# Softmax shift written into the score banks by ScalarE, negative means on GpSimd, new step orders and banks: a fused convolution-attention and transformer kernel

## The chip, the cores and the metric

One Trainium2 chip, one of its cores. The time is the device time of one execution in microseconds (us). TensorE (PE, with PEld for its weight loads), VectorE (DVE), ScalarE (ACT), GpSimd (POOL) and SyncE (SP) run their own instruction queues in order and meet at semaphores. The Python source was written with the step order of each engine as a table.

## The reference

32 images of 128 channels and 32x32 positions (1024 tokens) run through three layers, each with a residual:

```python
# L0: group norm, then attention over all 1024 tokens of an image, one head of 128
h = group_norm(x, gn_w, gn_b)
q, k, v = split(einsum('oc,bcn->bon', qkv_w, h) + qkv_b)
attn = softmax(einsum('bcn,bcm->bnm', q, k) * C ** (-0.5), axis=-1)
x = x + (proj_w @ einsum('bcm,bnm->bcn', v, attn) + proj_b)
# L1: layer norm, attention in windows of 32 tokens with 8 heads, out-projection,
#     layer norm, relu(x @ w1.T + b1) @ w2.T + b2, layer norm, residual
t = t + L1_attn(layer_norm(t))
# L2: layer norm, quantise to fp8 e4m3, matmul with a quantised kernel, bias, residual
t = t + L1_ffn(layer_norm(t))
```

The change touches the softmax of the first attention: its scores are shifted by the row maximum before the exponential.

## The kernel before

An image is worked on in two halves of 512 tokens. Each engine has a list of steps `name:half` in `PROGRAM`; `-` and `--` after a step say that it works for the image one or two iterations back, so three images are in flight at once. `@b` in TensorE's list names the PSUM bank (0 to 5) of the step's output; banks 6 and 7 hold the accumulators of the global products (`PV_BANKS`). The tables repeat per image: TensorE's as a loop of the hardware, the others written out. Before a TensorE step writes into its bank, `claim` (L861) waits for the semaphore with which the bank's last holder was read out (`RELEASE`, L97). In this table the order is written by hand or by a planner outside of the kernel; nothing is decided at run time, and an engine whose next step waits holds up all steps behind it.

The softmax of the global attention, for each image:

- `max:0` to `max:15` (TensorE L939, VectorE L710): rough scores, query-major, in one fp16 matmul of 128x512; VectorE takes the row maximum. Eight of them cover a half of the queries.
- `maxima:h` (VectorE L712): reduces them to `cmax`, one value per query, and splits it into a bf16 high and low part in columns 0 and 1 of `cparts`.
- `shift:h` (TensorE L942): turns `cparts` in four bf16 transposes, so that rows 0 and 1 hold the two parts for 512 queries; ScalarE (L519) copies these two rows into `shift`, whose other rows are zero.
- `st:0` to `st:15` (L952): one score tile each, keys on the partitions, 512 queries along the row. TensorE first multiplies `minus` (all -1) with `shift` (L962), which puts the negative maximum into the bank, and adds three matmuls of fp16 high and low halves (`three`, L873 to L877). ScalarE's `st` (L524) takes the exponential into one of four `p32` buffers (`PRING`).
- `pv:0` to `pv:15` (L966): fp32 products of `p32` with the values, four of 128x129 each; the profile records each of these twice. The last one of a half lets VectorE add the residual (`t`, L740).

Layer norms are VectorE's `variance` (L744: statistics, mean and variance, then epsilon in `veps`, then the negative mean `nmean`), GpSimd's `power` (L382: `rstd` by `pow`, then `nshift`), and four passes of ScalarE (`normalise`, L498), after which TensorE turns the result (`turn_in`, `turn_mid`). There are eight per image. Projections, window attention and the feed-forward part go in the same pattern: TensorE writes a bank, ScalarE reads out a high half in fp16 (`qh`, `xh`, `kk`, `oh`), VectorE the low half (`ql`, `xl`, `ol`), TensorE uses both.

## Time and profile before

| | |
|---|---|
| time, median of 3 runs | 2333.63 us (2331.12 to 2341.1) |
| the profiled execution, its own time | 2340.18 us |
| its span | 2338.4 us |
| TensorE busy | 2203.6 us, 94% |
| VectorE busy | 1748.5 us, 75% |
| ScalarE busy | 1476.5 us, 63% |
| GpSimd busy | 1219.1 us, 52% |
| granted TensorE clock, mean | 0.986 |

The busy time of an engine is that in which any of its instructions runs. TensorE's matmuls overlap: a row of 512 columns is shown with 0.38 us, but the next starts after 0.215 us, so the spacing of starts is what a matmul costs in a dense stretch. An idle time in square brackets is that of the engine in front of the row, with what ended it.

### The profile page before, as it was taken

To read this page: it belongs to the slowest core of one execution; us is meant where nothing else is said; L and a number is where in the kernel's file an instruction comes from. 1 tells how busy PE (TensorE), PEld (TensorE's weight loads), DVE (VectorE), ACT (ScalarE), POOL (GpSimd) and SP (SyncE) were. 2 spreads that over 40 slices of the span, in tenths; PEclk is the share of its full clock that TensorE was granted. 3 is DMA by queue.
4 is the path that set the end of the run, shared out by engine and by line. 5 is a ranking of instruction groups with operands and counts; after the bars stand their busy time and mean duration, and the time that the engine had idled before them with its cause. 6 is when DMAs were issued, how large, how long until landed. Compare 5 with 4: busy or idle time off the path is not lost.

```text
span 2338.4 us, 59675 instructions
## 1 busy us (share of the span) xinstructions
PE 2203.6 (94%) x21902; PEld 1605.9 (69%) x21902; DVE 1748.5 (75%) x5668; ACT 1476.5 (63%) x2881; POOL 1219.1 (52%) x1323
## 2 busy tenths in 40 slices
PE   4899999999999999999999999999999999999974
PEld 3677766677776677776677777677777677767653
DVE  5677787777787877787777787777787787787753
ACT  2566666766666666666766666666666666666653
POOL 5255444555444555444555454555555555555544
PEclk8999999999999999999999999999999999999997
DMA  1111111111111111111111111111111111111110
GB/s 44 29 36 30 45 38 45 30 40 29 44 37 45 29 41 30 44 37 45 36 36 31 43 36 45 42 31 34 39 36 45 44 28 38 34 36 45 37 28 19
DMA packets 76181, 86.79 MB, mean 37 GB/s; under 512 B 20624, under 2 KB 55440, under 8 KB 76048
## 3 DMA queue, kind: packets, MB, share of 16 engines
q1 hardware_dynamic: 62368, 52.44, 9.4%
q10 hardware_dynamic: 13680, 33.04, 4.2%
q14 instruction: 106, 0.87, 0.1%
q8 instruction: 27, 0.44, 0.1%
HBM read 18.29 MB, written 16.78 MB: 15 GB/s over the span
## 4 chain that ended last, share of the span: by engine, by line
PE 77%; ACT 7%; DVE 6%; issue 4%; SPq 2%; DMA 2%; POOL 2%; ACTq 0%; POOLq 0%; DVEq 0%
PE ps L981 16%; PE ps L875 10%; PE ps L1077 9%; PE ps L877 9%; PE ps L876 9%; PE ps L1045 5%; PE ps L962 4%; PE ps L939 4%; PE ps L1027 4%; PE ps L993 2%; ACT y L498 2%; SPq L328 2%; PE ps L928 1%; PE ps L1097 1%; DMA ptbd<-et 1%
## 5 line engine op out<-in xcount | busy, mean ns | idle before, releaser
L981 PEld LDWEIGHTS ps<-vg,p 128*128 128x128 f32 x4096 | 506.1, 192 | 40.5 <-issue 6.4
L385 POOL TENSOR_TENSOR rstd<-veps,halfpow 128x4 f32<-128x4 f32 x256 | 260.0, 1016 | 508.5 <-DVE veps L755 508.5
L981 PE MATMUL ps<-vg,p 128*128 128x129 f32 x4096 | 523.6, 277 | 0.9 <-ACT p L529 0.9
L529 ACT ACTIVATE p<-ps 128x512 f32<-128x512 f32 x512 | 292.1, 589 | 143.0 <-PE ps L877 113.0
L710 DVE TENSOR_REDUCE cm<-ps 128x1 f32<-128x512 f32 x512 | 334.9, 680 | 16.5 <-PE ps L939 16.3
L419 POOL TENSOR_TENSOR e<-e,srec 128x512 f32<-128x512 f32 x128 | 134.2, 1049 | 246.2 <-DVE srec L798 246.0
L1077 PE MATMUL ps<-w,hid 128*128 128x128 f32 x2048 | 241.7, 276 | 1.8 <-ACT hid L581 1.7
L1077 PEld LDWEIGHTS ps<-w,hid 128*128 128x128 f32 x2048 | 236.2, 192 | 7.6 <-issue 1.8
L581 ACT ACTIVATE hid<-ps,cols 128x512 f32<-128x512 f32 x256 | 165.9, 685 | 97.0 <-PE ps L877 96.9
L939 PE MATMUL ps<-kgh,qgh 128*128 128x512 f16 x512 | 175.8, 384 | 28.6 <-DVE qgl L704 22.3
L962 PE MATMUL ps<-shift,minus 128*128 128x512 bf16 x512 | 194.5, 380 | 2.0
L876 PE MATMUL ps<-qgl,kgh 128*128 128x512 f16 x512 | 194.5, 380 | 0.0
L875 PE MATMUL ps<-qgh,kgh 128*128 128x512 f16 x512 | 194.5, 380 | 0.0
L877 PE MATMUL ps<-qgh,kgl 128*128 128x512 f16 x512 | 194.4, 380 | 0.0
L403 POOL TENSOR_TENSOR y<-y,rows 128x512 f32<-128x512 f32 x64 | 81.6, 1275 | 133.5 <-PE ps L993 133.5
L572 ACT ACTIVATE oh<-ps 128x512 f16<-128x512 f32 x64 | 38.2, 597 | 178.2 <-PE ps L1045 178.2
L765 DVE TENSOR_TENSOR xl<-ps,xh 128x512 f16<-128x512 f32 x128 | 88.5, 692 | 76.9 <-ACT xh L537 76.8
L829 DVE TENSOR_TENSOR w<-ps,res 128x512 f32<-128x512 f32 x64 | 44.3, 692 | 127.4 <-PE ps L1077 124.3
L1045 PE MATMUL ps<-ptbd,v 128*32 128x128 f32 x4096 | 134.1, 277 | 3.0 <-DMA ptbd<-et 2.5
L498 ACT ACTIVATE y<-y,nshift,rstd 128x128 f32<-128x128 f32 x256 | 105.1, 482 | 42.8 <-POOL nshift L392 42.8
L498 ACT ACTIVATE z<-u,nshift,rstd 128x128 f32<-128x128 f32 x256 | 105.1, 482 | 35.9 <-POOL nshift L392 35.9
L1045 PEld LDWEIGHTS ps<-ptbd,v 128*32 128x32 f32 x4096 | 107.2, 111 | 26.2 <-DMA ptbd<-et 11.4
(184 smaller groups left out, 5504.3 us busy)
## 6 DMA issues: line engine op xcount, KB each, us to landing
ptbd<-et SPq DMA_DIRECT2D x512, 64.0 KB, 2.1
kbd<-kk SPq DMA_DIRECT2D x512, 32.0 KB, 2.0
out_y<-o_sb ACTq DMA_DIRECT2D x64, 256.0 KB, 2.4
x_sb<-in_x ACTq DMA_DIRECT2D x31, 512.0 KB, 4.0
x_sb<-in_x SPq DMA_DIRECT2D x1, 512.0 KB, 3.4
e<-in_w_t SPq DMA_DIRECT2D x1, 256.0 KB, 3.3
w<-in_w_t SPq DMA_DIRECT2D x1, 256.0 KB, 3.2
hid<-in_in_w_t SPq DMA_DIRECT2D x1, 192.0 KB, 2.6
```

The source lines that it names most:

```text
L385: g.tensor_tensor(rstd[:, k, h, :], veps[:, k, h, :], halfpow[:], ALU.pow).then_inc(s[f"ln_pow{k}"], 1)
L498: last = sc.activation(dst[:, h, P * j:P * (j + 1)] if dst is z else dst[:, h, j, :], src[:, h, j, :], ACT.Identity, bias=nshift[:, k, h, ...
L529: sc.activation(p32[:, c % PRING, :], bank("st", c), ACT.Exp, scale=C ** -0.5).then_inc(s["p_made"], 1)
L710: v_.reduce_max(cm[:, c // 2, c % 2:c % 2 + 1], bank("max", c), X).then_inc(s["max_out"], 1)
L875: mm(dst, lhi, rhi, start=first, stop=False, **kw)
L876: mm(dst, lhi, rlo, start=False, stop=False, **kw)
L877: return mm(dst, llo, rhi, start=False, stop=last, **kw)
L939: mm(bank("max", c), qgh[:, P * (c // 2):P * (c // 2 + 1)], kgh[:, HALF * (c % 2):HALF * (c % 2 + 1)], start=True, stop=True).then_inc(s[" ...
L962: mm(bank("st", c), minus[:], shift[:, h, :], start=True, stop=False)
L981: last = mm(ps[:, b, at:at + PVW], p32[:, c % PRING, part], vg32[:, j, :], start=j == 0 and q % 2 == 0, stop=j == MT - 1, skip_group_check ...
L1045: last = mm(ps[WIN * two:WIN * (two + 1), BANK["pv0", h], P * j:P * (j + 1)], v32[:, h, odd, j, WIN * two:WIN * (two + 1)], ptbd[:, h, j, ...
L1077: last = mm(bank("down", h)[:, part], hid[:, f, part], w2[:, f, :], start=f == 0, stop=f == FT - 1)
```

## The change

1. **Shift.** `maxima` is the reduction to `cmax` alone. `shift:h` turns each column of `cmax`, spread over 128 columns, in fp32 (four transposes), so that every partition holds the maxima of the 512 queries. ScalarE copies the whole bank, negated, into `shift`, now fp32 with 128 rows.
2. **Seeds.** A new step of ScalarE, `seed:c`, copies `shift` into the bank of score tile `c`. `st:c` on TensorE waits for it and adds its three matmuls, none of which starts the bank afresh; the matmul with `minus` is gone. Score tiles have banks 0 and 1 to themselves, in turn; a seed waits until the exponential of the tile two before has been taken. All other steps share banks 2 to 5. Once at the start two fp32 matmuls write to banks 0 and 1.
3. **Negative means.** `nmean` is computed by GpSimd at the head of `power`, instead of by VectorE behind `veps`.
4. **Orders and banks.** All tables of `PROGRAM` are new.

```diff
 PV_BANKS = (6, 7)
+ST_BANKS = (0, 1)
 PROGRAM = {
     "pe": """
-        max:7@3- turn_x:0@4- v:1@5-- out:0@2-- q:1@1-- shift:0@0- turn_x:1@3- max:8@2- st:0@4- max:9@0- st:1@3-
+        shift:0@5- out:0@2-- turn_x:0@3- max:9@5- st:0@0- st:1@1- max:10@4- pv:0- score0:1@2-- score1:1@5-- st:2@0-
...
+def seeded_over(c):
+    if c >= len(ST_BANKS):
+        return 0, c - len(ST_BANKS)
+    return 1, max(d for d in range(2 * MT) if d % len(ST_BANKS) == c)
...
-        cparts = sb("cparts", [P, HT, P], BF16)
-        shift = sb("shift", [P, 2, HALF], BF16)
+        shift = sb("shift", [P, 2, HALF])
...
             def power(n, k, h):
+                pool.wait_ge(s[f"ln_mv{k}"], upto(n))
+                g.tensor_scalar(nmean[:, k, h, :], mv[:, k, h, :, 0], -1.0, None, ALU.mult).then_inc(s[f"ln_mean{k}"], 1)
                 pool.wait_ge(s[f"ln_veps{k}"], upto(n))
...
             def make_shift(kind, img, c):
                 act.wait_ge(s["shift_turned"], upto(img, c + 1, per=2))
-                sc.activation(shift[0:2, c, :], bank("shift", c)[0:2, 0:HALF // 2].bitcast(BF16),
-                              ACT.Copy).then_inc(s["shift_made"], 1)
+                sc.activation(shift[:, c, :], bank("shift", c), ACT.Copy, scale=-1.0).then_inc(s["shift_made"], 1)
+
+            def seed(kind, img, c):
+                act.wait_ge(s["shift_made"], upto(img, c // MT + 1, per=2))
+                back, last = seeded_over(c)
+                if due(value := upto(img - back, last + 1, per=2 * MT)):
+                    act.wait_ge(s["p_made"], value)
+                sc.activation(bank("st", c), shift[:, c // MT, :], ACT.Copy).then_inc(s["seed_made"], 1)
...
-                v_.reduce_max(cmax[:], cm[:, HT * c:HT * (c + 1), :], X).then_inc(s["cmax_made"], 1)
-                dve.wait_ge(s["cmax_made"], upto(img, c + 1, per=2))
                 if due(value := upto(img, c, per=2)):
                     dve.wait_ge(s["shift_turned"], value)
-                v_.tensor_copy(cparts[:, :, 0], cmax[:]).then_inc(s["chi_made"], 1)
-                dve.wait_ge(s["chi_made"], upto(img, c + 1, per=2))
-                v_.tensor_tensor(cparts[:, :, 1], cmax[:], cparts[:, :, 0], ALU.subtract).then_inc(s["cparts_made"], 1)
+                v_.reduce_max(cmax[:], cm[:, HT * c:HT * (c + 1), :], X).then_inc(s["cmax_made"], 1)
...
-                v_.tensor_scalar(nmean[:, k, h, :], mv[:, k, h, :, 0], -1.0, None, ALU.mult).then_inc(s[f"ln_mean{k}"], 1)
...
+                if isinstance(img, int) and img == 0 and c == 0:
+                    pe.wait_ge(s["const_made"], 6)
+                    for b in ST_BANKS:
+                        mm(ps[:, b, :], identf[:], vg32[:].rearrange("p a b -> p (a b)")[:, 0:HALF], start=True, stop=True)
                 for q in range(HT):
-                    last = nc.tensor.transpose(dst[:, P * q:P * (q + 1)], cparts[:, q, :], identh[:])
+                    last = nc.tensor.transpose(bank("shift", c)[:, P * q:P * (q + 1)], cmax[:, q:q + 1].to_broadcast([P, P]),
+                                               identf[:])
...
             def st(kind, img, c):
                 h, j = divmod(c, MT)
-                claim(kind, img, "st", c)
+                pe.wait_ge(s["seed_made"], upto(img, c + 1, per=2 * MT))
...
-                mm(bank("st", c), minus[:], shift[:, h, :], start=True, stop=False)
                 three(bank("st", c), kgh[:, keys], kgl[:, keys], qgh[:, queries], qgl[:, queries],
-                      first=False).then_inc(s["st_mm"], 1)
+                      first=False, skip_group_check=True).then_inc(s["st_mm"], 1)
```

Three places of the new order. A row is a line of the kernel (of its own version), an instruction, and out<-in by the names of the code; `ps` is PSUM.

TensorE in the loop, from behind the turn of the first half's maxima to the first global product; before (L939 is `max`, L962 with `minus`, L875 to L877 the three matmuls of a score tile, L981 `pv`):

```order
L939 MATMUL ps<-kgh,qgh 128x512
L962 MATMUL ps<-shift,minus 128x512
L875 MATMUL ps<-qgh,kgh 128x512
L876 MATMUL ps<-qgl,kgh 128x512
L877 MATMUL ps<-qgh,kgl 128x512
L939 MATMUL ps<-kgh,qgh 128x512
```

And now (L949 is `max`, L993 `pv`):

```order
L949 MATMUL ps<-kgh,qgh 128x512
L885 MATMUL ps<-qgh,kgh 128x512
L886 MATMUL ps<-qgl,kgh 128x512
L887 MATMUL ps<-qgh,kgl 128x512
L885 MATMUL ps<-qgh,kgh 128x512
L886 MATMUL ps<-qgl,kgh 128x512
L887 MATMUL ps<-qgh,kgl 128x512
L949 MATMUL ps<-kgh,qgh 128x512
L993 MATMUL ps<-vg,p 128x129 x4
```

The first two score tiles now follow each other, each one matmul shorter, and a single `max` stands between them and the first product.

ScalarE at the same place; before (L521 the copy of the shift, L487 the turned x, L542 `qh`, L529 the exponential of a score tile, L561 the values, L498 a normalisation):

```order
L521 ACTIVATE shift<-ps 2x512
L487 ACTIVATE xt<-ps 128x512
L542 ACTIVATE qh<-ps,cols 128x512
L529 ACTIVATE p<-ps 128x512
L561 ACTIVATE v<-ps 128x16x16 x2
L529 ACTIVATE p<-ps 128x512
L498 ACTIVATE y<-y,nshift,rstd 128x128 x4
```

And now (L530 the shift, L537 a seed, L544 the exponential, L496 the turned x, L507 a normalisation):

```order
L557 ACTIVATE qh<-ps,cols 128x512
L530 ACTIVATE shift<-ps 128x512
L537 ACTIVATE ps<-shift 128x512 x2
L544 ACTIVATE p<-ps 128x512
L537 ACTIVATE ps<-shift 128x512
L544 ACTIVATE p<-ps 128x512
L537 ACTIVATE ps<-shift 128x512
L496 ACTIVATE xt<-ps 128x512
L507 ACTIVATE y<-y,nshift,rstd 128x128 x4
```

Two seeds stand behind the shift, then a seed behind each of the first exponentials; `qh` has moved ahead of the shift, the values behind.

VectorE ahead of the same turn; before (L710 a row maximum, L779 `kk`, L812 `ol`, L715 to L722 the maxima step, L818 the residual of the out-projection):

```order
L710 TENSOR_REDUCE cm<-ps 128x1 x3
L779 SCALAR_TENSOR_TENSOR kk<-ps,cols,kk 128x512
L710 TENSOR_REDUCE cm<-ps 128x1
L812 TENSOR_TENSOR ol<-ps,oh 128x512
L710 TENSOR_REDUCE cm<-ps 128x1
L715 TENSOR_REDUCE cmax<-cm 128x4
L720 CAST cparts<-cmax 128x4
L722 TENSOR_TENSOR cparts<-cmax,cparts 128x4
```

And now (L719 `kgl`, L725 a row maximum, L789 `kk`, L733 the maxima step, L822 `ol`):

```order
L719 SCALAR_TENSOR_TENSOR kgl<-ps,cols,kgh 128x512
L725 TENSOR_REDUCE cm<-ps 128x1 x2
L789 SCALAR_TENSOR_TENSOR kk<-ps,cols,kk 128x512
L725 TENSOR_REDUCE cm<-ps 128x1 x4
L733 TENSOR_REDUCE cmax<-cm 128x4
L822 TENSOR_TENSOR ol<-ps,oh 128x512
```

The last four row maxima follow each other, the maxima step is one instruction, and `ol` comes behind it.

## Rows read from the trace of the kernel before

**Rows 1.** Page, part 1: busy us of each engine (share of the span), instructions.

```profile
PE 2203.6 (94%) x21902; PEld 1605.9 (69%) x21902; DVE 1748.5 (75%) x5668; ACT 1476.5 (63%) x2881; POOL 1219.1 (52%) x1323
```

**Rows 2.** Windows: length, PE PEld DVE ACT POOL busy, clock; timeline, one image apart.

```profile
1004.00:1073.86 69.86, 68.15 (x686) 49.78 (x684) 53.94 (x177) 46.04 (x91) 37.22 (x41) 1.00 0.14 38
...
1004.41 0.30 PE L1097 MATMUL ps<-identf,u 128*128 128x128 f32 x1 [0.17 <-ACT qt L586]
1074.27 0.30 PE L1097 MATMUL ps<-identf,u 128*128 128x128 f32 x1 [0.17 <-ACT qt L586]
```

**Rows 3.** Timeline, TensorE, first score tile: start us, us, engine, line, operation, tiles, count.

```profile
1016.23 0.38 PE L939 MATMUL ps<-kgh,qgh 128*128 128x512 f16 x1
...
1016.67 0.38 PE L962 MATMUL ps<-shift,minus 128*128 128x512 bf16 x1
1016.88 0.38 PE L875 MATMUL ps<-qgh,kgh 128*128 128x512 f16 x1
...
1017.53 0.38 PE L939 MATMUL ps<-kgh,qgh 128*128 128x512 f16 x1
```

**Rows 4.** Timeline, TensorE: four bf16 turns, four fp32 turns, the next step.

```profile
1041.83 0.39 PE L947 MATMUL ps<-identh,cparts 128*128 128x128 bf16 x4
1042.05 0.60 PE L993 MATMUL ps<-identf,y 128*128 128x128 f32 x4
1042.49 2.04 PE L981 MATMUL ps<-vg,p 128*128 128x129 f32 x16
```

**Rows 5.** Page, part 5: the matmul with minus; count, busy us, mean ns.

```profile
L962 PE MATMUL ps<-shift,minus 128*128 128x512 bf16 x512 | 194.5, 380 | 2.0
```

**Rows 6.** Timeline, ScalarE behind the shift; page, part 5: Exp from SBUF to SBUF.

```profile
1015.98 0.59 ACT L521 ACTIVATE shift<-ps 2x512 bf16<-2x512 bf16 x1 [1.73 <-PE ps L947]
1016.48 0.57 ACT L487 ACTIVATE xt<-ps 128x512 f32<-128x512 f32 x1
...
L567 ACT ACTIVATE e<-e 128x512 f32<-128x512 f32 x128 | 80.4, 628 | 42.3 <-DVE e L788 41.9
```

**Rows 7.** Timeline, VectorE: the maxima step and the next; the negative mean and the next.

```profile
1014.73 0.16 DVE L715 TENSOR_REDUCE cmax<-cm 128x4 f32<-128x8 f32 x1
...
1015.22 0.69 DVE L818 TENSOR_TENSOR y<-ps,y 128x512 f32<-128x512 f32 x1
...
1017.35 0.16 DVE L756 TENSOR_SCALAR nmean<-mv 128x4 f32<-128x4 f32 x1
1017.42 1.28 DVE L710 TENSOR_REDUCE cm<-ps 128x1 f32<-128x512 f32 x2
```

**Rows 8.** Lines: GpSimd's nshift; count, busy us, mean ns, idle us before.

```profile
L392 POOL TENSOR_TENSOR nshift<-nmean,rstd 128x4 f32<-128x4 f32 x256 | 53.7, 210 | 20.2 <-POOL rstd L389 0.2
```

**Rows 9.** Timeline and window: last global products of an image to the next turn of maxima.

```profile
1067.01 2.95 PE L981 MATMUL ps<-vg,p 128*128 128x129 f32 x24
1069.79 0.22 PE L875 MATMUL ps<-wh,hh 128*128 128x128 f16 x1
...
1080.22 1.88 DVE L710 TENSOR_REDUCE cm<-ps 128x1 f32<-128x512 f32 x3
1082.01 0.75 DVE L779 SCALAR_TENSOR_TENSOR kk<-ps,cols,kk 128x512 f16<-128x512 f32 x1
1082.68 0.68 DVE L710 TENSOR_REDUCE cm<-ps 128x1 f32<-128x512 f32 x1
...
1085.42 0.39 PE L947 MATMUL ps<-identh,cparts 128*128 128x128 bf16 x4
...
1069.79:1085.42 15.63, 14.24 (x176) 9.37 (x174) 14.98 (x41) 10.38 (x20) 7.07 (x7) 1.00 0.21 56
```

**Rows 10.** Timeline, TensorE's waits in such a stretch; line L498, what its waits ended with.

```profile
1006.33 0.82 PE L939 MATMUL ps<-kgh,qgh 128*128 128x512 f16 x3 [0.61 <-DVE qgl L704]
1008.43 0.66 PE L993 MATMUL ps<-identf,y 128*128 128x128 f32 x4 [0.61 <-ACT y L498]
...
  POOL nshift L392: 90.6, 70
```

More of the change, by code:

```diff
@@ L63 @@
-    "act": """
-        vg:1- bias_x:0- k:1-- pv1:0-- turn_x:0- shift:0- turn_x:1- q:1-- st:0- v:1-- st:1- norm_mid:0-- turn_mid:0--
-        score0:1-- up0:0-- st:2- score1:1-- up1:0-- up2:0-- up3:0-- load_x:0 st:3- st:4- pv1:1-- st:5- norm_out:0--
-        st:6- norm_mid:1-- shift:1- st:7- turn_mid:1-- up0:1-- up1:1-- up2:1-- up3:1-- quant:0-- st:8- norm_in:0-
-        st:9- turn_in:0- st:10- norm_out:1-- k:0- turn_q:0-- st:11- st:12- ffn:0-- q:0- quant:1-- gn2:0 st:13-
-        st:14- st:15- score0:0- score1:0- kg:0 vg:0 kg:1 qg:0 turn_q:1-- v:0- qg:1 ffn:1-- norm_in:1- turn_in:1-""",
+        vg:1@2- max:2@5- k:1@4-- max:3@3- pv0:0@2-- max:4@5- max:5@3- max:6@4- pv1:0-- max:7@5- max:8@3- q:1@4--
@@ new lines @@
+        shift:0@5- out:0@2-- turn_x:0@3- max:9@5- st:0@0- st:1@1- max:10@4- pv:0- score0:1@2-- score1:1@5-- st:2@0-
+        pv:1- turn_mid:0@3-- st:3@1- max:11@2- max:12@5- v:1@4-- up0:0@3-- up1:0@2-- up2:0@4-- up3:0@3-- st:4@0-
+        turn_x:1@4- down:0@3-- pv0:1@4-- pv1:1-- st:5@1- pv:2- out:1@2-- pv:3- max:13@5- st:6@0- max:14@2- pv:4-
+        st:7@1- max:15@4- pv:5- pv:6- turn_mid:1@5-- shift:1@3- pv:7- up0:1@3-- up1:1@4-- up2:1@5-- up3:1@2--
+        st:8@0- gn1:0@5 down:1@2-- pv:8- st:9@1- turn_in:0@3- st:10@0- pv:9- gn2:0@3 k:0@2- st:11@1- v:0@4- pv:10-
@@ new lines @@
+        st:12@0- q:0@4- pv:11- st:13@1- pv:12- pv:13- st:14@0- st:15@1- turn_q:0@2-- score0:0@5- score1:0@4- pv:14-
+        pv:15- ffn:0@2-- kg:0@4 qg:0@3 turn_q:1@2-- qg:1@5 ffn:1@2-- vg:0@2 max:0@4 kg:1@3 turn_in:1@4- max:1@5""",
+    "dve": """
+        ln_in:1-- kg:0- qg:0- turn_p0:0-- prob1:0-- max:0- qg:1- turn_p1:0-- max:1- turn_in:1-- kg:1- max:2- max:3-
+        k:1-- max:4- max:5- max:6- max:7- maxima:0- pv1:0-- max:8- q:1-- out:0-- max:9- max:10- score0:1--
+        score1:1-- prob0:1-- turn_mid:0-- max:11- turn_p0:1-- prob1:1-- turn_p1:1-- max:12- down:0-- pv1:1-- out:1--
+        max:13- gn0:0 max:14- max:15- maxima:1- turn_mid:1-- ln_q:0-- pv:7- ln_in:0- quant:0-- down:1-- gn1:0
+        turn_in:0- k:0- ln_q:1-- q:0- gn2:0 quant:1-- score0:0- score1:0- pv:15- prob0:0-""",
@@ new lines @@
+    "act": """
+        k:1-- pv1:0-- q:1-- shift:0- seed:0- seed:1- st:0- seed:2- st:1- seed:3- turn_x:0- norm_mid:0-- score0:1--
+        st:2- turn_mid:0-- seed:4- st:3- score1:1-- v:1-- up0:0-- up1:0-- up2:0-- up3:0-- seed:5- st:4- turn_x:1-
+        load_x:0 pv1:1-- seed:6- st:5- seed:7- norm_out:0-- st:6- norm_mid:1-- st:7- turn_mid:1-- shift:1- seed:8-
+        seed:9- up0:1-- up1:1-- up2:1-- up3:1-- quant:0-- st:8- seed:10- norm_in:0- st:9- turn_in:0- st:10- seed:11-
+        norm_out:1-- k:0- seed:12- st:11- v:0- st:12- seed:13- q:0- seed:14- st:13- seed:15- quant:1-- gn2:0 st:14-
+        turn_q:0-- st:15- score0:0- score1:0- ffn:0-- kg:0 turn_q:1-- qg:0 qg:1 ffn:1-- norm_in:1- kg:1 vg:0
+        turn_in:1- bias_x:0 vg:1""",
@@ L69 @@
     "pool": """
-        prob1:1-- keep:1-- norm_mid:0-- down:0-- out:1-- norm_out:0-- norm_mid:1-- ln_q:0-- ln_in:0- quant:0--
-        down:1-- norm_out:1-- bias_out:0- ln_q:1-- gn2:0 quant:1-- prob0:0- prob1:0- ln_in:1- bias_out:1- keep:0-
-        out:0- prob0:1-""",
+        prob1:0-- bias_out:1-- keep:0-- out:0-- prob0:1-- prob1:1-- norm_mid:0-- keep:1-- down:0-- out:1--
+        norm_out:0-- norm_mid:1-- ln_q:0-- ln_in:0- quant:0-- down:1-- bias_out:0- norm_out:1-- ln_q:1-- gn2:0
+        quant:1-- prob0:0- ln_in:1-""",
@@ L348, in prologue @@
             def prologue():
[L349 removed]
+                for tile, value in ((identf, 0.0), (identh, 0.0), (group_mean, 1.0 / GROUP), (halfpow, -0.5)):
                     g.memset(tile[:], value).then_inc(s["const_made"], 1)
[L351 removed]
+                pool.wait_ge(s["const_made"], 4)
                 for tile in (identf, identh):
@@ L361, in prologue @@
                                 pattern=[[GROUP, P // GROUP], [0, GROUP]], channel_multiplier=-1).then_inc(s["const_mask"], 1)
-                for tile, value in ((cparts[:], 0.0), (vg32[:], 1.0), (ones, 1.0), (shift[:], 0.0)):
+                for tile, value in ((vg32[:], 1.0), (ones, 1.0)):
                     g.memset(tile, value).then_inc(s["const_made"], 1)
```

32 lines of the change are left out of this document (7 added, 25 removed).

## The prediction

> **What bounds the kernel now.** I read the shares of busy time first: TensorE is busy 94% of the span, VectorE 75%, ScalarE 63%, GpSimd 52% [rows 1]. The loop over the 32 images is steady: the same fp32 turn of the last step starts 69.86 us after its like one image earlier [rows 2], and in that one image TensorE is busy 68.15 of 69.86 us, VectorE 53.94, ScalarE 46.04 and GpSimd 37.22, at the full granted clock (1.00). So the period of one image sets the time, and TensorE's own work sets most of the period. Busy time there includes the tails of matmuls, so I also look at starts: TensorE does wait in one stretch, between the last product of an image's global attention (its last start is before 1069.79) and the turn of the next image's row maxima (1085.42) [rows 9]. Inside the same stretch of the period before stand waits for VectorE's low half of the queries and for ScalarE's normalisation, 0.61 us each as shown beyond the tails [rows 10]. VectorE is busy 14.98 of these 15.63 us [rows 9]. So: one stretch of about 15.6 us bound by VectorE, and some 54 us bound by TensorE.
>
> **TensorE loses one matmul per score tile.** Matmuls of 512 columns in one chain start 0.215 us apart: 1016.67, 1016.88, and four of them until 1017.53 [rows 3]. The tile's matmul with `minus` is one of these four; there are 512 [rows 5]. Per image 16 x 0.215 = 3.44 us go. They lie on TensorE, mostly in the stretch where TensorE itself is the bound, so this is time off the path.
>
> **The turn of the maxima becomes fp32.** Four bf16 turns take 0.22 us (1041.83 to 1042.05), four fp32 turns 0.44 us (1042.05 to 1042.49) [rows 4]. Two such steps per image: +0.44 us. In sum TensorE has 3.44 - 0.44 = 3.0 us less to do per image, 96 us over 32 images. Trainium skill, "FP8 and Floating Point Precision", section "TensorE Precision Notes", says that true FP32 takes four passes through the array. Four times the bf16 turn would be 0.88 us for a step, so +1.32 us per image instead of +0.44, 28 us in all; the fp32 turns of [rows 4] show twice, not four times.
>
> The new turns read one column spread over 128 (stride 0) as the stationary operand; no row shows that. The load of weights overlaps the matmul before it, so below I leave it at nothing, above at a doubled step: +0.9 us per image. The two fp32 matmuls at the set-up come once and cost under 2 us.
>
> **ScalarE gets 16 seeds per image.** A seed reads fp32 in SBUF and writes 128x512 fp32 to a PSUM bank. ScalarE writing PSUM isn't in the trace. The nearest rows: a 128x512 pass out of PSUM started 0.50 us before the next (1015.98, 1016.48), the Exp from SBUF to SBUF takes 0.628 us [rows 6]. I take 0.50, nearer in kind (a Copy of this width, queued back to back), and keep 0.63 as the upper end and 0.45 as the lower. 16 x 0.50 = 8.0 us (7.2 to 10.1). ScalarE goes from 46.0 to about 54 (53 to 56) of some 67 us, 80 to 84%: covered by TensorE as long as each seed is out when its bank is needed. If that cover is gone, 8 us a period lie bare. The Trainium skill, "ScalarE: Activation LUTs", section "Step-by-step: what each stage is for", says that ScalarE writes faster to PSUM than to SBUF; no row here shows it, and it would only make the seeds cheaper. The copy of the shift itself stays one instruction; 128 partitions instead of 2 cost the same, since the row with 2 partitions takes 0.59 like the full ones [rows 6].
>
> **VectorE loses small things.** The maxima step's three links take from 1014.73 to the next instruction at 1015.22 [rows 7], 0.49 us; one is left, some 0.1: two steps save 0.8 us per image. The negated mean costs 0.07 us from its start to the next one (1017.35, 1017.42) [rows 7], eight per image: 0.56. Together 1.4 us of 53.9.
>
> **GpSimd gets the negated mean**, 8 per image at 0.21 us (`nshift` has the same size) [rows 8], 1.7 us on an engine with 37.2 of 69.9. It now stands ahead of the `pow`. It starts with the mean and variance, while VectorE still adds epsilon, which covers about 0.17 of it; I take +0.1 us on each normalisation's chain, 0 to 0.25 as bounds. Only those that TensorE waits for matter (two or three per image), 0.2 us; what is queued behind a GpSimd wait is the next chain or the products of that half, which have room.
>
> **The new orders, walked.** I laid the new order of each engine out with starts and spacings of the old trace (0.50 per ScalarE pass [rows 6], 0.60 per row maximum and 0.67 per low half [rows 9], 0.1 to 0.2 per hand-over), from the last product of an image on.
> - The VectorE stretch. Between that product and the turn of the maxima VectorE has: the residual 1.25, two probability sums 1.74, the statistics 1.34, four low halves 2.6, two transposes 1.2, one `xl` 0.6, one `kk` 0.66, eight row maxima 4.8, the maxima 0.2, sum 14.4, with a few tenths of waiting 14.7; before, the same account gives 15.0, the trace 14.98 [rows 9]. So the stretch takes about 15.0 instead of 15.63 us. But the new order puts only about 11.9 us of TensorE's work there, where the old one had about 13.3. The waiting grows by about 0.8 us. Banks add nothing new to that in my walk, although all other tiles now share four banks: `max:3`, `vg:1` and `k:1` wait for banks 3, 2 and 4 within the same waiting.
> - Shift, seed, first tile. From the end of the turn to the first score tile: hand-over 0.2, shift 0.5 to 0.6, seed 0.5 to 0.6, 0.1, in sum 1.5. TensorE has out-projection 0.67, turn of x 0.45, one row maximum 0.22 between, 1.34. A wait of 0.2; the old order waited as long for the shift (the maximum at 1016.23 is followed by the tile at 1016.67, 0.22 late) [rows 3].
> - The other seeds stand ahead of their tile by the time of other steps on both engines. I find 0.15 us at `st:12` (behind a normalisation and a key step on ScalarE), 0.15 at `out:1`, nothing at `down:0`, and about 0.3 at `up0:1` as before. Against it the old wait of `turn_mid:0`, 0.3, goes, since more of TensorE's work stands ahead of it.
> Sum per image: 69.86 - 3.0 + 0.8 + 0.3 - 0.3 - 0.2 (tenths recovered where VectorE is shorter) = 67.45, about 67.4. Over 32 images 2.46 x 32 = 79 us. Start and end of the span stay. From the profiled run's own 2340.18 us (span 2338.4 and 1.8 around it) that gives 2261. The median of the runs before stands 0.28% lower (2333.63), so the forecast is 2255.
>
> **Rivals.**
> 1. **All of it.** The whole of TensorE's saving comes through: waits as before, 66.86 per image, 2340.2 - 96 = 2244, by the median 2238. For it: ScalarE has 20% free and the steps stand far from their seeds. Against it: the stretch that VectorE sets [rows 9]. With the waits even smaller it may reach 2225. Chance 0.17.
> 2. **Half of it.** VectorE's stretch and the four shared banks take another 1.0 to 1.5 us per image, 68.4 to 68.9, or 2287 to 2303. For it: a walk finds too few collisions, and a ScalarE at over 80% gives banks back later. Against it: outside the stretch the steps have other work between them. Chance 0.15.
> 3. **Slower.** Score tiles wait for seeds stuck in ScalarE's queue. ScalarE already sits idle before its normalisations waiting for GpSimd's `nshift`, 90.6 us in all [rows 10], 2.8 us per image, and now seeds for later tiles stand behind exactly these (`norm_out:1` ahead of `seed:12`, `norm_in:0` between `seed:10` and `seed:11`). TensorE stands at the tile, and with it all that is queued behind. Break-even is 3.0 / 16 = 0.19 us per tile; measurably slower from 0.21. At 0.25 us per tile the period is 69.86 + 4.0 - 3.0 = 70.9, the time 2340 + 32 = 2372, by the median 2366. Against it: most seeds are placed a whole tile or more ahead. Chance 0.07 for slower, 0.05 for the zone of no change.
> 4. **Dear turns.** The new turns cost what fp32 products do: 24 records, two to a matmul, in 2.78 us are 0.23 us each [rows 9], against 0.11 for a turn. 8 x 0.12 = 0.96 more per image, 31 us, 2286. For it: the spread column is a new operand. Against it: the same fp32 turn of other data [rows 4]. Chance 0.03. The Trainium skill's rule above would give nearly the same.
> 5. **The forecast,** 2240 to 2285: 0.53.
>
> **How the numbers follow.** About 0.5% is what a measurement of this kernel can tell from no change, 2322 to 2345. Faster: 0.53 + 0.17 + 0.15 + 0.03 = 0.88; within: 0.05; slower: 0.07. The range takes in rivals 1 and 2 and the bounds of seeds and turns: 2225 to 2305.
>
> **What would show it.** TensorE's records fall by 512, its busy time by 90 to 100 us; the seeds' row shows 512 passes of 0.55 to 0.63 us; ScalarE's busy time is near 1750 us, VectorE's near 1700; the period is 67 to 68 us; the stretch from the last product to the turn stays near 15 us and carries the longest waits; fp32 turns are spaced 0.11. Wrong would be: waits of score tiles for seeds of over 1 us per image in sum, seeds over 0.8 us, a granted clock under 1.00 in the loop, or a stretch over 16 us.

## The result, and the profile after it

The changed kernel takes 2315.05 us (median of 4 runs, 2311.32 to 2316.24); the kernel before, on the same chip, 2337.24. The ratio is 0.990, interval [0.988, 0.992]: faster by 22 us. The prediction was 2255, in 2225 to 2305. The direction was right; three quarters of the gain did not come, and the time lies above the range.

The page of the changed kernel, part 1, answers to [rows 1]:

```profile
PE 2141.3 (93%) x21394; PEld 1563.5 (68%) x21394; DVE 1698.6 (73%) x5284; ACT 1736.7 (75%) x3393; POOL 1272.5 (55%) x1576
```

TensorE has lost 508 records and 62.3 us of busy time, VectorE 50 us, ScalarE has gained 260: the work changed as forecast. Now the period, the time from the turn of the first half's maxima to the same turn one image later. Its median over the images is 69.30 us where it was 69.86. The first row below is one image of the changed kernel from turn to turn (length, then busy us of PE, PEld, DVE, ACT, POOL, clock), the second its stretch from the last global product of an image to the turn, as in [rows 9]:

```profile
1074.07:1143.35 69.28, 66.27 (x669) 48.55 (x669) 52.36 (x165) 54.13 (x107) 38.95 (x48) 1.00 0.14 38
1127.74:1143.35 15.61, 13.35 (x150) 7.45 (x148) 15.24 (x38) 10.39 (x19) 8.46 (x9) 1.00 0.26 73
```

The period fell by 0.56 us and not by 2.46. The stretch is 15.61 us in the median and not 15.0; it was 15.63. The rest of an image, between the turn and that last product, is 53.69 and was 54.23. I summed TensorE's starts to the next start over one image, each operation at its own usual spacing: its work did fall by 3.0 us, and what lies beyond the spacings rose by 2.4. The waits are new ones. TensorE's in the changed kernel (us in all, times, longest):

```profile
PE ps L1005 <- ACT y L507: 26.6, 33, 5.5
PE ps L885 <- ACT o_sb L609: 23.4, 30, 0.8
PE ps L885 <- DVE xl L775: 16.1, 64, 1.5
PE ps L1057 <- DMA ptbd<-et: 14.6, 29, 1.8
PE ps L1109 <- ACT qt L601: 13.1, 4, 11.3
PE ps L1098 <- POOL qz L438: 11.8, 30, 1.8
```

Before, the longest of these that came in every image were `y` 30.4 and `qgl` 22.3 us. `qgl` is gone; in its place `vg:0` waits in each image until ScalarE has read `ffn:1` out of the same bank (`o_sb`), 0.8 us, the probabilities' DMA (`ptbd`) and GpSimd's `qz` take 0.4 to 0.5 each, and the low half `xl` takes 0.25 twice in each image, where it had one wait in the whole run. Only once in 512 tiles did TensorE stand idle for a seed, 0.4 us.

### The profile page after: what moved, and what is told of

It reads as the page before. It is cut to its first block and busy times, and to the rows that moved or that the text cites. A ratio compares the mean times of both kernels' runs of the same rounds, so it can differ in the third digit from the quotient of the medians.

```text
span 2314.5 us, 59631 instructions
## 1 busy us (share of the span) xinstructions
PE 2141.3 (93%) x21394; PEld 1563.5 (68%) x21394; DVE 1698.6 (73%) x5284; ACT 1736.7 (75%) x3393; POOL 1272.5 (55%) x1576
## 5 line engine op out<-in xcount | busy, mean ns | idle before, releaser
L993 PEld LDWEIGHTS ps<-vg,p 128*128 128x128 f32 x4096 | 511.5, 192 | 51.9 <-issue 12.9
L993 PE MATMUL ps<-vg,p 128*128 128x129 f32 x4096 | 537.9, 278 | 0.7 <-ACT p L544 0.7
L392 POOL TENSOR_SCALAR nmean<-mv 128x4 f32<-128x4 f32 x256 | 58.3, 228 | 575.3 <-DVE mv L763 572.0
L544 ACT ACTIVATE p<-ps 128x512 f32<-128x512 f32 x512 | 300.2, 587 | 91.1 <-PE ps L887 90.6
L725 DVE TENSOR_REDUCE cm<-ps 128x1 f32<-128x512 f32 x512 | 334.0, 679 | 15.5 <-PE ps L949 13.9
L537 ACT ACTIVATE ps<-shift 128x512 f32<-128x512 f32 x512 | 300.9, 596 | 17.4 <-ACT p L544 0.7
L394 POOL TENSOR_TENSOR rstd<-veps,halfpow 128x4 f32<-128x4 f32 x256 | 265.8, 1038 | 0.0
L949 PE MATMUL ps<-kgh,qgh 128*128 128x512 f16 x512 | 176.8, 382 | 3.3 <-DVE kgl L719 1.6
L507 ACT ACTIVATE y<-y,nshift,rstd 128x128 f32<-128x128 f32 x256 | 105.2, 483 | 45.9 <-POOL nshift L401 45.9
L817 DVE STREAM_TRANSPOSE et<-e 128x512 f32<-128x512 f32 x128 | 90.4, 706 | 39.6 <-POOL e L428 38.9
```

What stands on the lines that cost most here:

```text
L394: g.tensor_tensor(rstd[:, k, h, :], veps[:, k, h, :], halfpow[:], ALU.pow).then_inc(s[f"ln_pow{k}"], 1)
L537: sc.activation(bank("st", c), shift[:, c // MT, :], ACT.Copy).then_inc(s["seed_made"], 1)
L544: sc.activation(p32[:, c % PRING, :], bank("st", c), ACT.Exp, scale=C ** -0.5).then_inc(s["p_made"], 1)
L725: v_.reduce_max(cm[:, c // 2, c % 2:c % 2 + 1], bank("max", c), X).then_inc(s["max_out"], 1)
L949: mm(bank("max", c), qgh[:, P * (c // 2):P * (c // 2 + 1)], kgh[:, HALF * (c % 2):HALF * (c % 2 + 1)], start=True, stop=True).then_inc(s[" ...
L993: last = mm(ps[:, b, at:at + PVW], p32[:, c % PRING, part], vg32[:, j, :], start=j == 0 and q % 2 == 0, stop=j == MT - 1, skip_group_check ...
```

## The experiments

Each was timed in three rounds beside the kernel before on its chip. "Ratio" is to the kernel before; the changed kernel has 0.990. The edits are against the changed kernel unless the kernel before is named. They are cut to what matters, and rows of `PROGRAM` are shown in part. Several runs test what their expectations call the ring or the section chain: the idea that a closed chain of hand-overs through all engines sets the period.

### Is TensorE the bound, or ScalarE with its seeds?

**Old order without `minus`** (kernel before):

```diff
-                mm(bank("st", c), minus[:], shift[:, h, :], start=True, stop=False)
                 three(bank("st", c), kgh[:, keys], kgl[:, keys], qgh[:, queries], qgl[:, queries],
-                      first=False).then_inc(s["st_mm"], 1)
+                      ).then_inc(s["st_mm"], 1)
```

> The kernel before, in its old order, with the matmul with minus left out of all 16 score tiles of an image (so the exponential is taken of unshifted scores); nothing else differs, ScalarE has no seeds. Theory of the section chain (mine now): an image's period is set by a ring of three pieces, the dense TensorE section from the turn of the first half's maxima to the end of down:1, then a chain of hand-overs through the norms and GpSimd to the last products, then VectorE's stretch. Only the 9 tiles st:0 to st:8 lie in the dense section, so at most 9 x 0.215 = 1.94 us per image come back, 45 to 62 us in all, ratio 0.973 to 0.981. Rival 'TensorE is the bound nearly everywhere and only the seeds or the new order cost': 16 x 0.215 x 32 = 110 us, ratio about 0.953.

2308.06 us, ratio 0.987 [0.986, 0.989]. Of 110 us of matmuls 30 come out as time. Both theories missed (45 to 62 us, or 110): whoever takes away TensorE's work alone, in the old order, gets about a quarter. The waits that grew against the kernel before are those for VectorE and for the keys' DMA (`kbd`, before 8.4 us, 7 times):

```profile
PE ps L939 <- DVE qgl L704: 27.9, 32, 1.6
PE ps L1026 <- DMA kbd<-kk: 23.2, 38, 4.0
```

**New order without seeds.** Three matmuls that start their bank afresh, no shift:

```diff
-"shift": make_shift, "seed": seed, "st": st
+"shift": make_shift, "st": st
-                pe.wait_ge(s["seed_made"], upto(img, c + 1, per=2 * MT))
+                claim(kind, img, "st", c)
...
-                      first=False, skip_group_check=True).then_inc(s["st_mm"], 1)
+                      ).then_inc(s["st_mm"], 1)
```

> The changed kernel without the 16 seeds (score tiles start their bank afresh and wait for the exponential of the tile two before instead; the scores stay unshifted). ScalarE has 8 us less per image. Section chain: the seeds stand in ScalarE's slack, at most 0.2 to 0.4 us per image come back, 2300 to 2312 us. Rival 'ScalarE's seeds ate the gain': most of the missing 60 us comes back, 2250 to 2270 us.

2312.53 us, 0.989 [0.988, 0.991]: all 512 seeds together cost about 3 us, which is within the noise. The rival with the seeds (3) is dead, and so is every story in which the 8 us of ScalarE's new work per image took the gain.

**One matmul less in the tiles `st:1` to `st:7`, or in `st:9` to `st:15`.** The edit of the first; the second has `c >= 9`:

```diff
+                if 1 <= c <= 7:
+                    mm(bank("st", c), kgh[:, keys], qgh[:, queries], start=False, stop=False, skip_group_check=True)
+                    mm(bank("st", c), kgl[:, keys], qgh[:, queries], start=False, stop=True,
+                       skip_group_check=True).then_inc(s["st_mm"], 1)
...
```

> The changed kernel with one of the three matmuls (the product with the low half of the queries) left out in st:1 to st:7, seven tiles in the dense TensorE section. 7 x 0.215 x 32 = 48 us less work for TensorE. Section chain: 30 to 48 us faster than the changed kernel, 2267 to 2285. Rival 'TensorE is off the path everywhere in the new order': under 10 us.

> The same with st:9 to st:15 instead, seven tiles behind down:1; TensorE's work falls by the same 48 us. Section chain: nothing, 0 to 8 us faster than the changed kernel, 2307 to 2316. If TensorE were the bound there too: 48 us faster, as in the run before.

2309.27 us (0.987 [0.986, 0.989]) and 2316.04 us (0.991 [0.989, 0.993]): 48 us of TensorE's work in either place are worth 6 us, not clear of the noise, and nothing. These tiles stand in "some 54 us bound by TensorE". The section chain had 30 to 48 us for the first of the two, and fell there; its rival, under 10, holds.

**One matmul more in each tile**, with zero weights:

```diff
+                mm(bank("st", c), zero[:], qgh[:, queries], start=False, stop=False, skip_group_check=True)
                 three(bank("st", c), kgh[:, keys], kgl[:, keys], qgh[:, queries], qgl[:, queries],
```

> The changed kernel with one matmul more in each score tile, of 128x512 with zero weights, so the result stays. It puts back 16 x 0.215 = 3.44 us of TensorE's work per image, 110 us in all, and nothing else of the old code. Theory A (TensorE's work is nearly on the path upwards, though taking more away brings nothing): 90 to 110 us slower than the changed kernel, ratio to before 1.028 to 1.037, so that nearly all of the 97 us between the old and the new code in the new order is this matmul. Theory B (the new order has slack of TensorE everywhere): under 50 us, ratio under 1.012, and the 97 us come mostly from the maxima step of VectorE.

2370.83 us, 1.014 [1.011, 1.017]: 110 us more of work cost 56. Between the two theories. So TensorE's work has a price of nothing to an eighth downwards and of half upwards: the changed kernel stands at a bend.

### Is it VectorE's row of maxima?

**Row maxima over half of the columns**, in the new order, in the old one, and in the old one without `minus`:

```diff
-                v_.reduce_max(cm[:, c // 2, c % 2:c % 2 + 1], bank("max", c), X).then_inc(s["max_out"], 1)
+                v_.reduce_max(cm[:, c // 2, c % 2:c % 2 + 1], bank("max", c)[:, 0:HALF // 2], X).then_inc(s["max_out"], 1)
```

> The changed kernel, but each row maximum of VectorE reads 256 of its 512 columns (the shift is then the maximum of half of the keys). VectorE's work falls by 16 x 0.27 = 4.3 us per image, 2.2 of it between the last product and the turn of the maxima; TensorE's and ScalarE's work is the same. The runs before showed that taking 1.5 us per image from TensorE gives 0.3 and 8 us from ScalarE 0.05. Theory of the ring: VectorE's unbroken row of work sets the stretch behind the last product, so 1.0 to 2.2 us per image come back, 2245 to 2285 us. Rival, TensorE or ScalarE set it: under 0.3 us per image, 2305 to 2315.

> The kernel before with the same halved row maxima, in the old order and with its matmul with minus. VectorE lighter by 4.3 us per image. If VectorE alone set the old order's period in its stretch, 1.0 to 2.0 us per image, 32 to 64 us faster than before (ratio 0.973 to 0.986). If TensorE set it, nothing (ratio 0.997 to 1.0).

> The kernel before with both cuts: no matmul with minus, halved row maxima. The matmul alone gave 0.93 us per image of its 3.44. If TensorE and VectorE hold the period together, the two cuts give more together than the sum of each alone: 3.0 us per image or more, ratio under 0.958. If a chain of hand-overs sets the rest, the sum stays about that of the two alone.

2296.48 (0.982 [0.980, 0.983]), 2333.95 (0.998 [0.997, 0.999]) and 2307.55 us (0.987 [0.985, 0.988]). VectorE's busy time falls by some 3.5 to 3.8 us per image each time (4.3 were expected). That brings 19 us in the new order, 4 in the old, and nothing in the old order once `minus` is gone. For the new order the 19 us, 0.55 per image, lie between the ring's 1.0 to 2.2 and its rival's 0.3. The window of one image of that last kernel (columns as above) still has TensorE busy 95%, with 3.44 us less to do; below it pieces of the chain of waits that ended last, in the same stretch (start, us, what):

```profile
2094.00:2162.85 68.85, 65.47 (x669) 48.29 (x668) 50.42 (x176) 45.66 (x91) 37.17 (x40) 1.00 0.14 38
```

```profile
2112.12 0.69 DVE xl L765
2112.81 0.60 DVE ssum L796
2113.44 0.26 DVE srec L798
2113.77 1.06 POOL e L419
2114.88 0.71 DVE et L807
2115.61 0.63 SPq L335
2116.28 0.61 SPq L335
2116.94 0.60 SPq L335
2117.58 4.08 DMA ptbd<-et
2121.80 1.95 PE ps L1044 x64
...
2130.09 0.90 DVE cparts L720
```

The chain goes through every engine and through the DMA: in one image of it, the 195 longest pieces sum to 32.1 us on TensorE, 15.8 on VectorE, 6.7 in transfers, 6.4 on ScalarE, 3.1 on SyncE, 1.6 on GpSimd. In the kernel before, the same sum over one image was 59.9 of some 68 us on TensorE. So a chain of hand-overs lay about 1 us per image behind TensorE's own: the period fell from 69.86 to 68.85 us and no further.

The last piece is one that the expectations did not count on. In the second half of each image the cast of the maxima step takes 0.89 us here, 0.54 in the old order without `minus` and 0.19 in the kernel before; it ends each time 0.03 us behind the same row of GpSimd. Where VectorE came to it sooner, it was held longer, and TensorE waited for the step at 30 turns (16.8 us, 12.3 of them at the start). That the lighter VectorE brought nothing there is in part this hold; how much of it, no run says.

**All three lighter** (no seeds, two of three matmuls in every tile, half maxima, as above):

> The changed kernel with all three engines lighter at once: no seeds (ScalarE 8 us per image less), two matmuls per score tile in all 16 (TensorE 3.44 less), halved row maxima (VectorE 4.3 less). Alone such cuts gave 0.05, 0.35 and 0.57 us per image. If two engines hold each other up (each relieved one meets the next), the three together give far more than the sum: 3 us per image or more, under 2225 us. If a ring of hand-overs of fixed latency holds the period: about the sum, 0.8 to 1.6 us per image, 2265 to 2290.

2284.38 us, 0.978 [0.975, 0.981]: 31 us below the changed kernel, about what the single effects sum to (3, 6 and 19), and in the ring's range. TensorE is busy 93% of an image even there, which shows how little that share tells; the window of one image, and TensorE's first waits:

```profile
1004.00:1072.25 68.25, 63.31 (x653) 46.84 (x652) 48.66 (x164) 45.71 (x91) 38.50 (x49) 1.00 0.14 39
...
PE ps L1041 <- DMA kbd<-kk: 41.7, 35, 2.6
PE ps L1007 <- ACT y L507: 41.0, 66, 5.5
```

### What the order costs, and what the code brings in it

**Old code in the new order** (kernel before, with all tables and banks of the changed one):

```diff
 PROGRAM = {
     "pe": """
-        max:1@1- max:2@2- max:3@0- vg:1@5- turn_in:1@3-- pv0:0@1-- max:4@2- max:5@5- k:1@4-- max:6@0- pv1:0--
+        vg:1@2- max:2@5- k:1@4-- max:3@3- pv0:0@2-- max:4@5- max:5@3- max:6@4- pv1:0-- max:7@5- max:8@3- q:1@4--
...
```

> The kernel before in all its code (matmul with minus, bf16 parts of the maximum, negative means on VectorE, no seeds), with the tables of orders and banks of the changed kernel. TensorE has 3.0 us more per image than the changed kernel, ScalarE 8 less, VectorE 1.4 more. If the new order only needs what the new code frees: slower than before, 71 to 72.5 us per image, ratio 1.01 to 1.035. If the new order is what makes the changed kernel faster and the seeds are worth little: 69.3 to 69.9, ratio 0.99 to 1.0.

2412.73 us, 1.032 [1.030, 1.034]. This is the run that splits the result: the new order by itself costs 75 us with the old code, and in the new order the new code is worth 98. Of the 2.4 us per image that the order costs, 2.3 lie outside of VectorE's stretch (56.49 against 54.23 us; the stretch is 15.73). That 98 is close to what the prediction counted on TensorE (96) is luck: much of it is not TensorE's work, as TensorE's longest wait shows:

```profile
PE ps L948 <- DVE cparts L723: 64.6, 63, 12.2
```

In the kernel before, TensorE waited for `cparts` once, at the start. Here it does so at 63 of the 64 turns, 0.8 us on average without the first. VectorE takes the maxima step right behind the last row maximum in both orders. In the kernel before, TensorE's other work just reached to the end of the step: the turn starts 0.24 to 0.26 us behind the last link, where the hand-over alone takes 0.15 in this run. In the new order TensorE comes too early at the first turn of an image (0.5 us), and at the second (1.2 us) the step is longer. VectorE and, below it, GpSimd at such a second turn (timeline):

```profile
1148.65 0.16 DVE L716 TENSOR_REDUCE cmax<-cm 128x4 f32<-128x8 f32 x1
1148.84 0.49 DVE L721 CAST cparts<-cmax 128x4 bf16<-128x4 f32 x1
1149.37 1.19 DVE L723 TENSOR_TENSOR cparts<-cmax,cparts 128x4 bf16<-128x4 f32 x1
...
1148.03 1.27 POOL L446 TENSOR_TENSOR u<-u,w 128x512 f32<-128x512 f32 x1
1149.26 1.26 POOL L412 TENSOR_TENSOR res<-y,rows 128x512 f32<-128x512 f32 x1
```

The cast ends with GpSimd's first row (1149.33 and 1149.30), the subtraction with its second (1150.56 and 1150.52). Each takes 0.18 us in the first half of an image, where no such row runs.

**The maxima step in three links**, in the changed kernel:

```diff
-                v_.reduce_max(cmax[:], cm[:, HT * c:HT * (c + 1), :], X).then_inc(s["cmax_made"], 1)
+                v_.reduce_max(cmax0[:], cm[:, HT * c:HT * (c + 1), :], X).then_inc(s["cm0_made"], 1)
+                dve.wait_ge(s["cm0_made"], upto(img, c + 1, per=2))
+                v_.tensor_copy(chi[:], cmax0[:]).then_inc(s["chi_made"], 1)
+                dve.wait_ge(s["chi_made"], upto(img, c + 1, per=2))
+                v_.tensor_tensor(cmax[:], cmax0[:], chi[:], ALU.max).then_inc(s["cmax_made"], 1)
```

> The changed kernel with the maxima step on VectorE in three links again (reduce, a cast of 128x4 to bf16, and a tensor_tensor of 128x4 with two operands in SBUF, here a maximum that leaves the shift valid). Nothing is left out. In the old code with the new order the last two links took 0.49 and 1.19 us in the second half of an image, while a 128x512 tensor_tensor of GpSimd ran, and TensorE waited 64.6 us for them. Theory A (the step is bare in the new order): they take the same here, the period grows by 0.5 to 1.7 us, ratio 0.997 to 1.014. Theory B (the freed TensorE time hides it): under 0.2 us per image, ratio 0.989 to 0.993.

2376.19 us, 1.017 [1.014, 1.019]: 61 us for 128 instructions that take 0.16 to 0.17 us each when nothing is in the way; the period is 71.03 us instead of 69.30, at the upper end of theory A. In the second half of an image they end with GpSimd's rows again (timeline, VectorE, GpSimd, and TensorE's turn that waits):

```profile
1061.72 0.59 DVE L736 CAST chi<-cmax 128x4 bf16<-128x4 f32 x1
1062.34 1.18 DVE L738 TENSOR_TENSOR cmax<-cmax,chi 128x4 f32<-128x4 f32 x1
...
1061.01 1.27 POOL L455 TENSOR_TENSOR u<-u,w 128x512 f32<-128x512 f32 x1
1062.24 1.26 POOL L421 TENSOR_TENSOR res<-y,rows 128x512 f32<-128x512 f32 x1
...
1063.67 0.62 PE L965 MATMUL ps<-identf,cmax 128*128 128x128 f32 x4 [1.50 <-DVE cmax L738]
```

So of the 98 us between the two codes the matmul alone is 56 and the maxima step alone 61. The two together were not run; if the rest of the new code (seeds, fp32 turns, means) is worth as little as the runs on it say, they overlap by about 20.

**`turn_x:0` moved into VectorE's stretch**, from behind the turn of the maxima to ahead of `pv1:0`:

```diff
-        pv0:0@2-- max:4@5- max:5@3- max:6@4- pv1:0-- max:7@5- max:8@3- q:1@4-- shift:0@5- out:0@2-- turn_x:0@3- max:9@5-
+        pv0:0@2-- max:4@5- turn_x:0@3- pv1:0-- max:5@3- max:6@4- max:7@5- max:8@3- q:1@4-- shift:0@5- out:0@2-- max:9@5-
```

> The changed kernel with one step moved: turn_x:0 from behind the turn of the maxima to ahead of it, between pv0:0 and pv1:0, where TensorE waits for VectorE anyway; ScalarE copies it there, in its 2.4 us of idle time, and no longer ahead of norm_mid:0. Nothing is left out. TensorE's dense piece from the turn of the maxima to turn_mid:0 (7.58 us) gets 0.45 shorter. Ring: 0.3 to 0.45 us per image faster, 2300 to 2306. If TensorE's place in the ring were not there (the runs that lightened it said 0.3 of 1.5): 0 to 0.1, 2312 to 2316.

2342.61 us, 1.003 [1.001, 1.004]: 28 us slower, where both theories had it faster. The stretch has no room even though TensorE idles in it. It is 16.74 us long instead of 15.61: the step takes a bank in turn, and TensorE waits for the row maxima to free the next. Besides, score tiles now do wait for a seed, 8.0 us in 32 times.

```profile
PE ps L936 <- DVE cm L712: 13.4, 34, 2.0
```

**`turn_mid:0` back to where the old order had it:**

```diff
-        score0:1@2-- score1:1@5-- st:2@0- pv:1- turn_mid:0@3-- st:3@1-
+        score0:1@2-- score1:1@5-- turn_mid:0@3-- st:2@0- pv:1- st:3@1-
     "act": """
-        seed:2- st:1- seed:3- turn_x:0- norm_mid:0-- score0:1-- st:2- turn_mid:0--
+        seed:2- st:1- turn_x:0- norm_mid:0-- seed:3- score0:1-- turn_mid:0-- st:2-
```

> The changed kernel with norm_mid:0 ahead of seed:3 on ScalarE and turn_mid:0 ahead of st:2 and pv:1 on TensorE, near to where the old order had it. Nothing is left out. In the changed kernel this turn starts 7.6 us after the turn of the maxima, in the kernel before 5.5. Theory A (the late turn_mid:0 is what the new order costs): it starts about 1 us earlier, down:0 too, and the period falls by 0.5 us or more, ratio under 0.985. Theory B (the stretch makes it up again, as it did when the score tiles behind it were made lighter): period within 0.3 us, ratio 0.986 to 0.995, with seed:3 later and TensorE waiting for the normalisation instead.

2337.04 us, 0.999 [0.998, 1.000], 22 us slower. The turn starts 7.06 us behind the turn of the maxima instead of 7.58, but now it is TensorE that waits, one time more per image (26.6 us, 33 times, in the changed kernel):

```profile
PE ps L992 <- ACT y L494: 58.1, 65, 5.5
```

The theory that the late place is the fault fell, and theory B, a period within 0.3 us, missed too. The late place suits the new order, perhaps because `out:0`, the head of that chain, comes behind the shift; that is not shown.

### Single hand-overs taken away

**`vg:0` behind `max:0` and `kg:1`; `vg:0` in the bank of `kg:0`** (banks 2 and 4 exchanged from there to `out:0`); **the first with the negative means on VectorE:**

```diff
-        ffn:1@2-- vg:0@2 max:0@4 kg:1@3 turn_in:1@4- max:1@5
+        ffn:1@2-- max:0@4 kg:1@3 vg:0@2 turn_in:1@4- max:1@5
```

```diff
-        ffn:1@2-- vg:0@2 max:0@4 kg:1@3 turn_in:1@4- max:1@5
+        ffn:1@2-- vg:0@4 max:0@2 kg:1@3 turn_in:1@2- max:1@5
```

> The changed kernel with one step of TensorE moved: vg:0, which waits in each image 0.78 to 0.94 us for ffn:1 to be read out of the same bank, comes behind max:0 and kg:1. Nothing is left out. Theory A (this new wait is where the gain went): the wait goes, the period falls by 0.8 us, 26 us in all, ratio to the kernel before near 0.979. Theory B (a ring of hand-overs: TensorE only arrives earlier at the next one, xl, qz, or the row maxima of VectorE): under 0.3 us per image, ratio 0.986 to 0.991, and the waits of other rows grow by about what this one loses.

> The changed kernel with the order kept and banks 2 and 4 exchanged from vg:0 to out:0, so that vg:0 gets the bank of kg:0 (free long before) and max:0, one step later, the bank of ffn:1. Nothing is left out. Theory A: about half of the wait goes (0.3 to 0.5 us per image), ratio 0.984 to 0.987. Theory B: under 0.2 us per image, ratio 0.988 to 0.991.

> The changed kernel with vg:0 behind max:0 and kg:1 and, besides, the negative means back on VectorE. Nothing is left out. If the two single effects add up (the second was 5 us alone): 5 us below the kernel with vg:0 moved alone. If TensorE and VectorE meet in the same hand-over at the row maxima, where VectorE's row is now the longer one, no gain beyond the kernel with vg:0 moved alone, or a loss of a few us, because the negated means (0.56 us per image) lie in VectorE's row.

2311.91 (0.990 [0.988, 0.993]), 2315.89 (0.991 [0.988, 0.993]) and 2312.88 us (0.990 [0.988, 0.993]); the period is 69.30, 69.28 and 69.22. The largest new wait, for `o_sb`, is gone from all three, and nothing is won, as theory B said. In the first it reappears at the next two hand-overs, 42.4 instead of 26.6 and 8.2 instead of 0.3, together what was taken away (23.4); in the second `y` has 47.3:

```profile
PE ps L998 <- ACT y L500: 42.4, 34, 5.5
...
PE ps L878 <- DVE qgl L712: 8.2, 31, 0.3
```

**Negative means back on VectorE; GpSimd's multiply with `RG2` left out:**

```diff
-                g.tensor_scalar(nmean[:, k, h, :], mv[:, k, h, :, 0], -1.0, None, ALU.mult).then_inc(s[f"ln_mean{k}"], 1)
+                v_.tensor_scalar(nmean[:, k, h, :], mv[:, k, h, :, 0], -1.0, None, ALU.mult).then_inc(s[f"ln_mean{k}"], 1)
```

```diff
-                g.tensor_tensor(w[:, h], w[:, h], row(RG2), ALU.mult).then_inc(s["t2a_made"], 1)
-                pool.wait_ge(s["t2a_made"], upto(n))
```

> The changed kernel with the negated mean back on VectorE behind veps, as before. VectorE has 0.56 us more per image, 0.2 of it in the stretch behind the last product; GpSimd 1.8 less, but its pow starts at the same time either way (0.25 us behind veps in both traces). Ring: 0.1 to 0.3 us per image slower, 2317 to 2325. If the move had lengthened the norms' chain: faster, 2300 to 2310.

> The changed kernel without GpSimd's multiplication of the second norm by its weight (1.27 us, twice per image; the result lacks that weight). GpSimd is busy only 55% of the span, so by busy time this is worth nothing. Ring of hand-overs: after down:1 its product is followed on GpSimd by the sum into u, then VectorE's statistics of u, and so on to the last products; one of the two multiplications stands in that chain, so up to 1.27 us per image come back, 0.5 to 1.3, 2275 to 2300 us. If the ring doesn't run through there: 2311 to 2317.

2310.33 (0.989 [0.986, 0.992]) and 2307.98 us (0.988 [0.985, 0.991]). The move of the means is worth nothing that can be told from zero: the loop's period is nearly the same (69.22), the 5 us in the profiled run lie ahead of the second turn of maxima at the start of the program (56.6 instead of 61.9 us). 1.27 us less on GpSimd per half image bring 7 us, between the ring's 16 to 42 and nothing.

None of the five stands clear of the changed kernel.

## Why the prediction was wrong, step by step

- **Removed work: right.** 3.44 and 0.44 us per image; TensorE's starts give 3.0. The fp32 turn takes 0.44 us (four turns at 1032.71, the next product at 1033.15), twice the bf16 turn of [rows 4], so the spread operand costs nothing and rival 4 is out. The rule of the Trainium skill, "FP8 and Floating Point Precision", section "TensorE Precision Notes", of four passes for fp32, is not borne out for turns; the fp32 products of [rows 9], 0.23 us each against 0.055 for a 16-bit one of 128 columns, do take four times as long.
- **Seeds: right in what matters.** 0.596 us each, 0.52 from start to start (two in 1.12); ScalarE is busy 75% of the span and 54.1 of 69.3 us in one image, as forecast. Without them 3 us less.
- **Negative means:** the +0.1 us on a normalisation's chain did not come; `rstd` starts 0.25 us behind `veps` in both kernels.
- **The step that failed first:** "one stretch of about 15.6 us bound by VectorE, and some 54 us bound by TensorE", and with it "mostly in the stretch where TensorE itself is the bound". A busy share near 94% and dense starts were taken for a bound. By the prediction's own terms these 54 us should have come down to 52.4 (67.4 less the stretch of 15.0); they came down from 54.23 to 53.69. The old order pays 30 us for 110 us of matmuls, the new one 6 and 0 for 48. Behind TensorE's row stood a chain through VectorE, GpSimd, SyncE, the transfers and ScalarE, about 1 us per image later, and [rows 10] had shown two of its waits in one place; the walk followed only the first tiles and the stretch, and held the rest for covered.
- **The new orders:** the sum gives them +0.8 us of waiting in the stretch and then tenths. With the old code they cost 75 us, 2.4 per image. The prediction never asked what the order does without the code. Where its own terms can be held against the trace: the stretch is 15.61 and not 15.0, with VectorE busy 15.24, 0.8 above the 14.4 of the walk, so 0.6 of the 1.9 us that are missing per image lie there. The other 1.3 lie outside of it, where the waits are hand-overs for which the sum has nothing (`vg:0` 0.8, `ptbd`, `qz` and `xl` 0.4 to 0.5 each).
- **VectorE's maxima step:** 0.4 us each, as work off a covered engine, and put into the sum as a tenth or two. In the new order TensorE stands idle for it, and in the second half of an image its two links are held by GpSimd's rows: 61 us. Without this piece the change would have been a loss: the kernel with three links takes 2376.
- **Start and end stay:** nearly. The third turn of maxima comes 1.8 us earlier, the end 3.7 us sooner behind the last turn: 5.5 of the 24 us between the two profiled spans.

Rival 2 had the right kind ("a walk finds too few collisions") and too small a size, 68.4 to 68.9 us per image against 69.30. That no single engine's work sets the period is shown by the runs that relieve one engine each (0 to 19 us) and by the one that relieves three (31, about their sum). That a closed ring of hand-overs sets it in its place is argued and not shown: of the forecasts made from it, those for the lighter score tiles, the lighter VectorE, the lighter GpSimd and the moved `turn_x:0` were too high or of the wrong sign. Which link would have to go first is open: the one new wait that was taken away came back next door. Of the order's 75 us only the waits for the maxima step are known, some 52 us without the one at the start; the rest is open.

## What to carry to other kernels

A high busy share is no bound. Before pricing removed work at its full length, follow the chain of waits of an image with that work taken out and ask what is late next; with in-order queues on five engines it may stand a percent behind (here 1 us of 70). When a change brings a new order along, price the order with the old code and the code in the old order apart: here they were +75 and -98 us, and neither could be seen in the -22. And look at what stands bare between the last producer and the turn: two instructions of 0.16 us per turn, 128 in all, were worth as much as 512 matmuls, because another engine held them at every second turn.
